# Transposing x on VectorE from a second, quartered load, in a language adapter followed by a category linear layer

## The reference

```
w1 = W1[lang[s]]  (512 x 128)     w2 = W2[lang[s]]  (128 x 512)     w = W[cat[s]]  (512 x 512)
h  = relu(x @ w1 + b1)                        # up projection
y  = x + h @ w2 + b2                          # down projection and residual
n  = (y - mean(y)) * rsqrt(var(y) + 1e-5)     # over the 512 features
x1 = x + n * gamma + beta
out = x1 + x1 @ w + b
```

## Time and profile before

| | |
|---|---|
| median of 3 runs | 688.96 us (687.92 to 689.35) |
| profiled execution, span from first to last instruction | 683.6 us |
| PE busy / VectorE / ScalarE / GpSimd | 667.4 / 545.6 / 505.0 / 446.6 us |
| DMA moved | 134.55 MB, mean 197 GB/s |

### The profile page before, as it was taken

One profiled execution on the slowest core, in us unless ns is written; L12 is line 12 of the kernel. 1 busy time (PEld: TensorE's weight loads), 2 busy tenths in 40 slices (PEclk: granted clock), 3 DMA queues, 4 the chain that ended last, 5 costly groups with the idle time before them and its releaser, 6 DMA issues.

```text
span 683.6 us, 12284 instructions
## 1 busy us (share of the span) xinstructions
PE 667.4 (98%) x3425; PEld 551.5 (81%) x3425; DVE 545.6 (80%) x1129; ACT 505.0 (74%) x992; POOL 446.6 (65%) x359
## 2 busy tenths in 40 slices
PE   8789999999999999999999999999999999999997
PEld 7668887888888888888888888888878888888885
DVE  2788888888888878888888887888888888887873
ACT  4777778877778787778787778877778887777850
POOL 4746776666776666876666777666777666777640
PEclk9999999999999999999999999999999999999999
DMA  7453665556665556666565675645675655675522
GB/s 239 164 187 122 218 200 217 186 181 229 215 217 206 189 174 228 215 224 206 187 205 192 215 245 186 215 175 192 215 246 188 206 207 174 221 233 191 182 88 94
DMA packets 67239, 134.55 MB, mean 197 GB/s; under 512 B 8770, under 2 KB 26268, under 8 KB 63260
## 3 DMA queue, kind: packets, MB, share of 16 engines
q1 hardware_dynamic: 67228, 134.43, 57.9%
HBM read 100.71 MB, written 33.55 MB: 196 GB/s over the span
## 4 chain that ended last, share of the span: by engine, by line
PE 78%; DVE 9%; ACT 6%; issue 4%; DMA 1%; SPq 1%; DVEq 0%
PE o_bank L668 14%; PE o_bank L669 14%; PE o_bank L670 14%; PE n_bank L706 8%; PE x_bank L695 7%; PE d_bank L668 6%; PE d_bank L670 5%; PE d_bank L669 5%; ACT norm L424 5%; DVE y L527 2%; DVE xT_lo L512 1%; DVE neg_mean L531 1%; PE x_bank L668 1%; PE x_bank L669 1%; PE x_bank L670 1%
## 5 line engine op out<-in xcount | busy, mean ns | idle before, releaser
L338 POOL TENSOR_TENSOR x_tok<-x_tok,b_bc 128x512 f32<-128x512 f32 x128 | 161.7, 1296 | 116.8 <-PE x_bank L695 116.8
L668 PE MATMUL o_bank<-w_hi,x1T_hi 128*128 128x512 f32 x512 | 209.2, 409 | 1.9 <-DVE x1T_lo L573 1.5
L670 PE MATMUL o_bank<-w_hi,x1T_lo 128*128 128x512 f32 x512 | 201.6, 394 | 0.0
L669 PE MATMUL o_bank<-w_lo,x1T_hi 128*128 128x512 f32 x512 | 200.4, 391 | 0.0
L344 POOL TENSOR_TENSOR w_lo<-w_raw,w_hi 128x512 fp32r<-128x512 f32 x128 | 163.0, 1307 | 9.4 <-ACT w_hi L403 9.4
L424 ACT ACTIVATE norm<-y,neg_mean 128x512 f32<-128x512 f32 x128 | 91.0, 713 | 67.8 <-DVE neg_mean L531 67.8
L670 PEld LDWEIGHTS o_bank<-w_hi,x1T_lo 128*128 128x128 f32 x512 | 96.3, 188 | 21.8
L668 PEld LDWEIGHTS o_bank<-w_hi,x1T_hi 128*128 128x128 f32 x512 | 96.7, 189 | 19.8 <-issue 1.8
L669 PEld LDWEIGHTS o_bank<-w_lo,x1T_hi 128*128 128x128 f32 x512 | 97.0, 189 | 18.2
L567 DVE SCALAR_TENSOR_TENSOR n_bank<-n_bank,params,xT_beta 128x512 f32<-128x512 f32 x126 | 91.9, 752 | 24.0 <-PE n_bank L706 24.0
L407 ACT ACTIVATE x1T_hi<-n_bank 128x512 fp32r<-128x512 f32 x126 | 75.6, 600 | 45.5 <-DVE n_bank L567 43.6
(11 more groups left out here) (80 smaller groups left out, 994.4 us busy)
## 6 DMA issues: line engine op xcount, KB each, us to landing
w_raw<-in_L_cond_W SPq DMA_DIRECT2D x32, 1024.0 KB, 5.3
out<-out_half SPq DMA_DIRECT2D x63, 512.0 KB, 3.0
x_tok<-in_x SPq DMA_DIRECT2D x31, 1024.0 KB, 4.9
w_raw<-in_L_cond_W SPq DMA_DIRECT2D x64, 256.0 KB, 5.4
b_bc<-in_L_cond_b SPq DMA_DIRECT2D x64, 256.0 KB, 6.6
x_tok<-in_x SPq DMA_DIRECT2D x2, 512.0 KB, 3.8
params<-param_table SPq DMA_DIRECT2D x32, 4.5 KB, 1.7
out<-out_half SPq DMA_DIRECT2D x2, 256.0 KB, 2.4
```

The lines of the kernel that those rows point to most:

```text
L338: pool.tensor_tensor(x_tok[p][:, t, :], x_tok[p][:, t, :], b2_bc[p][:, :], ALU.add).then_inc(x_b2_done, 1)
L668: pe.matmul(acc, lhs_hi, rhs_hi, start=first, stop=False)
L669: pe.matmul(acc, lhs_hi, rhs_lo, start=False, stop=False)
L670: return pe.matmul(acc, lhs_lo, rhs_hi, start=False, stop=last)
```

## The change

x is loaded twice. `x_tok` now holds token 128t+p in tile t on partition p. A second copy, `x_quad`, comes by four DMAs, one for each quarter (32 partitions), each a quarter of the features in blocks of 32 tokens, in runs of 512 bytes. DVE transposes it in 32x32 blocks, one instruction per chunk, into `xT` in SBUF. Chunk c thereby holds features q*128+c*32+i; the rows of W1 and W (four DMAs each instead of one), gamma, beta, and the columns of norm are put into the same order. PE no longer transposes x, and the banks `x_bank` serve the down projection alone.

ACT makes xT_hi from SBUF in two instructions of 128x1024. DVE makes xT_lo of chunks 0 and 1, POOL that of chunks 2 and 3. `xT_beta` is gone: x1 adds `xT`, beta is the bias of x1T_hi on ACT and is added in low_x1 on DVE (with a per-partition scalar). The diagonal of w is added in four instructions. The parameter load waits for low_x1 instead of x1, and the load of w stands behind it. PE's up waits for the low parts by chunk.

```diff
+            def load_x_quads(s, p):
+                for n in range(NQ):
+                    sp.dma_start(x_quad[p][quad(n), :, :],
+                                 x_quads[bass.ds(s, 1), n].rearrange("o j b f -> j (o b) f")
+                                 ).then_inc(xq_in[p], 16)
...
+                    load_x_quads(k.sample(-1), q)
+                    load_w12(lang, q)
                     load_x(k.sample(-1), q)
-                    load_w12(lang, q)
...
-                        sp.wait_ge(x1_done, k.count(NC, 0, 0))
+                        sp.wait_ge(x1_lo_done, k.count(NC, 0, 0))
                     load_params(lang, q)
...
+            def low_xT(k, c):                      # POOL
+                pool.wait_ge(xT_hi_done, k.count(2, 0, 2))
+                pool.tensor_tensor(xT_lo[:, c, :], xT[k.p][:, c, :], xT_hi[:, c, :].bitcast(F32),
+                                   ALU.subtract).then_inc(xT_lo_pool_done, 1)
...
+                    for c in range(NC):
+                        block = chunk_columns(w_raw[q][:, c, :], c)
+                        pool.tensor_tensor(block, block, ident[:, :].rearrange("p (q i) -> p q i", q=NQ),
+                                           ALU.add).then_inc(diag_done, 1)
+                if adapter:
+                    low_xT(k, 2)
+                    low_xT(k, 3)
...
+            def high_xT(k, i):                     # ACT
+                act.wait_ge(xT_done, k.count(NC, 0, 2 * i + 2))
+                if i == 0 and k.since(1):
+                    act.wait_ge(up_done, k.count(1, 0, 0))
+                act.activation(xT_hi[:, 2 * i:2 * i + 2, :], xT[k.p][:, 2 * i:2 * i + 2, :], ACT.Copy
+                               ).then_inc(xT_hi_done, 1)
...
                 if adapter:
-                    copy_xT(k, 0)
-                    copy_xT(k, 1)
+                    high_xT(k, 0)
                 normalise(k, 0)
                 normalise(k, 1)
                 if adapter:
-                    copy_xT(k, 2)
-                    copy_xT(k, 3)
+                    high_xT(k, 1)
                 high_w(k)
...
+            def turn_x(k, c):                      # DVE
+                if c == 0:
+                    dve.wait_ge(xq_in[k.p], 16 * NQ * k.pairs(0) + 16 * NQ)
+                dve.transpose(xT[k.p][:, c, :].rearrange("p (b j) -> p b j", j=SQ),
+                              x_quad[k.p][:, :, c * SQ:(c + 1) * SQ]).then_inc(xT_done, 1)
...
                 if adapter:
-                    low_xT(k, 0)
-                    low_xT(k, 1)
+                    turn_x(k, 0)
+                    turn_x(k, 1)
                 normalise(k, 2)
                 normalise(k, 3)
                 output(k, 0)
                 if adapter:
-                    low_xT(k, 2)
-                    low_xT(k, 3)
+                    turn_x(k, 2)
+                    turn_x(k, 3)
+                if adapter:
+                    low_xT(k, 0)
+                    low_xT(k, 1)
                 output(k, 1)
...
             def step(h, p):                        # PE
                 k = Step(h, p)
-                turn_x(k, 0)
-                turn_x(k, 1)
                 linear_tile(k, 0)
-                turn_x(k, 2)
-                turn_x(k, 3)
                 linear_tile(k, 1)
```

More of the change, by code:

```diff
@@ L84, in adapter_then_conditional_linear @@
         params = [sb(f"params{i}", [P, NP]) for i in range(2)]
+        x_quad = [sb(f"x_quad{i}", [P, NB, NC * SQ]) for i in range(2)]
+        xT = [sb(f"xT{i}", [P, NC, T]) for i in range(2)]
         xT_hi = sb("xT_hi", [P, NC, T], F32R)
         xT_lo = sb("xT_lo", [P, NC, T], F32R)
-        xT_beta = [sb(f"xT_beta{i}", [P, NC, T]) for i in range(2)]
         w1_hi = [sb(f"w1_hi{i}", [P, NC, A], F32R) for i in range(2)]
@@ L120, in adapter_then_conditional_linear @@
         ids = sb("ids", [1, 2, S], I32)
-        param_rows = sb("param_rows", [L * NP, P])
+        param_rows = norm[0:L, :, :].rearrange("l t h -> l (t h)")
         param_table = sb("param_table", [P, L, NP])
-        x_bank = [bank(f"x_bank{i}") for i in range(2)]
+        y_bank = [bank(f"y_bank{i}") for i in range(2)]
         n_bank = [bank(f"n_bank{i}") for i in range(2)]
@@ L144, in adapter_then_conditional_linear @@
         rows_in = sem("rows_in")
-        x0_left_in = sem("x0_left_in")
+        xq_in = [sem(f"xq_in{i}") for i in range(2)]
         x_in = [sem(f"x_in{i}") for i in range(2)]
@@ L155, in adapter_then_conditional_linear @@
         table_turned = sem("table_turned")
-        xT_done = sem("xT_done")
         up_done = sem("up_done")
@@ L223, in load_w @@
             def load_w(g, p):
-                sp.dma_start(w_raw[p][:, :, :], w_rows[bass.ds(g, 1)].rearrange("o p c h -> p (o c) h")
-                             ).then_inc(w_in[p], 16)
+                for n in range(NQ):
+                    sp.dma_start(w_raw[p][quad(n), :, :],
+                                 w_rows[bass.ds(g, 1), n].rearrange("o i c h -> i (o c) h")
+                                 ).then_inc(w_in[p], 16)
             def load_b(g, p):
@@ L393, in normalise @@
                         act.wait_ge(nT_done, k.count(NC, 1, 0))
-                act.activation(norm[:, t, :], y[:, t, :], ACT.Identity, scale=rstd[:, t:t + 1],
+                act.activation(by_chunk(norm[:, t, :]), by_quad(y[:, t, :]), ACT.Identity, scale=rstd[:, t:t + 1],
                                bias=neg_mean_rstd[:, t:t + 1]).then_inc(norm_act_done, 1)
@@ L451, in step @@
                     deviation(k)
+            for c in range(NC):
+                for rows, at in ((gamma, c * P), (beta, H + c * P)):
+                    act.dma_start(param_rows[:, at:at + P].rearrange("l (q i) -> l q i", q=NQ),
+                                  chunk_columns(rows, c)).then_inc(rows_in, 16)
+            act.dma_start(param_rows[:, 2 * H:2 * H + A], b1).then_inc(rows_in, 16)
             act.wait_ge(ident_done, 2)
@@ L458, in _ @@
             k0, k1 = Step(0, 0), Step(0, 1)
-            for c in range(NC):
-                act.wait_ge(xT_done, c + 1)
-                act.activation(xT_hi[:, c, :], xT_bank(k0, c)[:, :], ACT.Copy).then_inc(first_xT_hi_done, 1)
-            for c in range(NC):
-                act.wait_ge(xT_lo_done, c + 1)
-                xT_plus_beta(k0, c)
+            high_xT(k0, 0)
+            high_xT(k0, 1)
+            high_w12(0, 0)
             relu(k0)
-            copy_xT(k1, 0)
-            copy_xT(k1, 1)
             high_w12_of_next(k0)
+            high_xT(k1, 0)
+            high_xT(k1, 1)
             deviation(k0)
-            copy_xT(k1, 2)
-            copy_xT(k1, 3)
             normalise(k1, 0)
@@ L557, in normalise @@
             def normalise(k, t):
-                dve.tensor_scalar(norm[:, t, :], y[:, t, :], rstd[:, t:t + 1], neg_mean_rstd[:, t:t + 1],
+                dve.tensor_scalar(by_chunk(norm[:, t, :]), by_quad(y[:, t, :]), rstd[:, t:t + 1], neg_mean_rstd[:, t:t + 1],
                                   ALU.mult, ALU.add).then_inc(norm_dve_done, 1)
```

213 lines of the change are left out of this document (90 added, 123 removed).

## The result

The changed kernel takes 879.0 us (median of four runs, 874.1 to 881.7) beside 689.2 us of the kernel before on the same chip (687.9 to 690.0): a ratio of 1.275, 95% interval 1.271 to 1.279. The forecast said slower, and 735 us; the time lies far above its range, which ended at 790. Where two executions of one kernel lie more than 1.5% apart, the text goes by the faster one.

A forecast was written before the change was run, and what follows sets the result against it. PE and a second path through DVE were taken to bound the kernel together; 30 steps of 0.8 us longer path plus 0.75 us POOL waits, 46 us, on 683.6 gave a 730 us span, 735 us median, range 684 to 790.

The forecast's parts named there:

- POOL in the way of DVE: Small DVE operations before rstd stand behind POOL's longer work: 0.75 us per step, bounds 0 and 1.5.
- The load of w: Issued behind low_x1(3) from D+3.1 to D+4.7, landed by D+8.5 to D+10, just in time for POOL: counted 0.
- The new path without POOL waits: From rstd through turns, copies, norms, linear tile 2 and down: 21.2 us per step instead of 20.4, +0.8.
- D+5.6: End of neg_mean_rstd, 5.6 us after D, where down has been issued and linear tile 3 starts; no turn starts earlier.
- The rival of the costly turn: A DVE turn of x costs twice an ordinary pass, 1.3 us: +2.7 us per step, 816 us; chance 0.06.
- The rival of the late load: Quarters of w written at half rate land 2 to 3 us later: step 23.0 us, 768 us; chance 0.06.
- The clock rival: PE's clock drops between D+8 and D+15, some eight matmuls dearer: 1.6 us per step, 783 us; chance 0.08.
- The signs of being wrong: PE without mid-step waits, turns well under 0.5 us, w_hi before D+11, idle POOL at rstd; low clock, late w for rivals.
- The prologue: Start of the kernel, about 43 us long, with changed loads and fillers: given 0, plus or minus 3 us.
- DMA, counted as hidden: x quarters, w1, w2 and the second x, 33.6 MB more at a mean of 230 GB/s: no cost.
- PE freed, 2.2 us per step: Transposes of x leave PE: 1.8 us of work and some 0.4 us of waits per step; PE alone needs 18.2.
- The faster rival: PE stays the bound if low_x1(1) ends before D+14.2: step 19.3 us, 657 us, least 623; chance 0.16.

The follow-up runs named there:

- the run with no hold left: Changed kernel with the load of w ahead of the wait for low_x1, neg_mean on ACT and POOL's four b2 additions left out: 694.0 us, ratio 1.011.

## Why the prediction was wrong

The step that failed is "POOL in the way of DVE": it priced the hold of a small DVE operation with one POOL operation, and the runs showed it standing to the end of POOL's run. The load of w, counted as 0, failed behind it.

- **What bounds the kernel before:** right. PE and a second path through DVE arrive together: the two kinds of small operations off DVE gave 1.6% and no more, with PE still at 98%.
- **The new path without POOL waits, 21.2 us:** roughly right. Its start D+5.6 still contained 0.6 us of a held neg_mean and 0.6 us of var_eps; without them it would be 20.0, and the run with no hold left gave 20.35. Its parts: turns come in pairs of 1.30 us (0.65 each, taken 0.64); xT_hi 1.06 (taken 1.1); POOL's xT_lo 1.28 (taken 1.3). The rival of the costly turn is out. The wait of PE for ACT's norm, predicted as 1.3 us or more, doesn't show in the changed kernel, where PE waits earlier, for DVE's output (127.6 us in the list above). With neg_mean on ACT it is there, 1.8 us in each of 29 steps:

```profile
PE n_bank L717 <- ACT norm L423: 51.2, 29, 2.2
```

- **"POOL in the way of DVE", 0.75 us per step, bounds 0 and 1.5:** this is the step that failed. It saw that neg_mean would fall into POOL's run, and even that the run would reach to D+5.3 (in the step shown it ended at D+5.2), but it counted "an operation of 0.17 us stands behind a whole POOL operation". neg_mean was passed over at four boundaries and lasted nearly five operations; and where the prediction named the second neg_mean, in about half of the steps it was the first, at D-0.4. neg_mean alone lost 150.3 - 64 x 0.17 = 139 us, 4.5 us per step. The kernel before had lost 0.6 us per step to it, so 3.9 us are new, over twice the upper bound. With neg_mean off DVE the step came to 22.2, near the forecast's 21.95, but in part by luck: var_eps lost 1.4 us there, twice the term. No row of the kernel before could show more than one operation: its largest neg_mean is 1287 ns. But the earlier trace rows show that POOL stopped for 2.5 and 4 us in each step there, and the working itself had noted that POOL's long run would now reach over neg_mean. The upper bound should have been the rest of that run, not one operation.
- **The load of w, counted 0:** wrong, in its start above all. In the step shown D is 414.05, where linear tile 3 starts. The load is issued at D+8.2 instead of D+3.1, and lands at D+15.1 instead of D+8.5 to D+10, since it waits for low_x1, which stands behind the held neg_mean on DVE. In the list of waits it is POOL's 271 us, and loading w first was worth some 50 us. The rival of the late load, with quarters at half the rate and 2 to 3 us later, isn't seen: the last quarter landed 5.3 us after its issue, the time that the prediction took. POOL's four diagonal parts took 2.6 us in the step shown instead of 1.3 to 1.6; DVE's xT_lo, with two inputs in SBUF, ran beside them there and was slowed too (0.95 us at most, 0.65 at least).
- **The clock rival:** its mechanism did occur, some nine matmuls at the 1.2 GHz level in the step shown, but as a result: the granted clock is 0.50 behind PE's wait of 5 us. Over the span it fell to 0.89; with the holds reduced it was 0.95 to 0.97, without any 0.985. The step fell by 4.2 us, from 26.4 to 22.2, when neg_mean left DVE; how much of that was the clock's wasn't measured by itself.
- **The signs of being wrong:** a clock under 0.95 was to be the clock rival, and POOL's diagonal waiting for w past D+11 the load rival. Both signs came true, and neither rival was the cause: the signs didn't tell a cause from what follows out of it. Changing one operation at a time did.
- **The prologue, 0 plus or minus 3 us:** too small. The first down projection starts 8.9 us later, a small part of the 189 us, but all of what the run without holds lost.
- **DMA, counted as hidden:** held for this kernel (share 70%). In the run without holds the queue's share is 88.7% of 692 us, with more and smaller packets than before (157636 against 67239), and a quarter of w lands 8.6 us after its issue instead of 4.3. So the loads may well be the next bound; that isn't shown.

```profile
q1 hardware_dynamic: 157204, 167.96, 88.7%
```

- **PE freed, 2.2 us per step:** PE's work did go, and none of it reached the end. The faster rival asked for low_x1(1) before D+14.2; with all these holds removed the step was only 0.1 us under the one before.
- By the SBUF — State Buffer page of the Trainium skill (SBUF: two separate sides) DVE and POOL share a pair of SBUF ports, and whoever starts first holds it for the whole instruction. The runs agree on which operations are held: a one-input `tensor_scalar` (neg_mean, var_eps), and one with two inputs in SBUF (newton, 1008 ns). They show more on how long: 5.69 us, until the fifth of POOL's operations had ended. The page speaks of one instruction and doesn't say who is served next; that this means one POOL operation was the prediction's own reading, and its middle between "not held" and "held once" couldn't reach the time measured.

What stays open: why the place in the run matters. The runs show that it does, on both kernels and with idle operations; they don't show what inside the chip keeps DVE's request from being served, nor a depth from which on that happens, nor what decides the even cases at the twelfth operation. No run added a bare stop of POOL, one that doesn't wait for DVE, and nothing else. It wasn't settled either why loading w first made things worse once neg_mean was on ACT.

## What to carry to other kernels

Before you lengthen or move GpSimd's work, look for its longest stretch without a stop and for the small VectorE operations with operands in SBUF that fall into it: take the rest of that stretch as the upper bound of what each can cost, not one operation. Then ask what stands behind them in the queues; if the start of the stretch itself waits for them, the loss repeats in every step. Two cheap cures each took back two thirds of the loss here: small statistics on ScalarE, or a wait of GpSimd for the small operation. And time freed on the bounding engine is worth only the distance to the second path; measure that path with its stalls taken out. Last, when you write down signs that would show a rival, ask whether they would also follow from another cause.

## What the runs showed of the hardware

- A VectorE operation of 0.17 us (128x2, SBUF to SBUF) was held 5.7 us, through four boundaries between GpSimd operations, and up to 7.3 us in another kernel. When it asked in the second, fourth or sixth operation after a stop of 0.04 to 0.17 us it was let in at the first boundary, 88 times of 88; passed over once in the changed kernel, it stood to the end of the run every time (28 of 28).
- The transposition in 32x32 blocks, SBUF to SBUF, 128x512 float32, has a mean of 687 ns. Most of these ran while GpSimd was idle; four that started inside GpSimd operations of 1.3 us, between 25 and 27 us, took 670 to 702 ns, so they were not held.
- Four idle operations per step, 4 us, on an engine busy 65% cost some 200 us of 687 in one place of its queue and 48 us in another.
